# Expert results added straight into the rows of the residual sums, and a last stage that only copies

## The reference, cut to what matters

```
out = x + attention(xn)                      # 16 heads of 16, causal, RoPE
        + shared(xn)                         # silu(xn @ sgate.T) * (xn @ sup.T) @ sdown.T
        + sum over 4 chosen experts of p_e * down_e( silu(gate_e(xn)) * up_e(xn) )
```

## Time and profile before

| | us |
|---|---|
| median of 3 runs (2672.46 to 2676.88) | 2676.68 |
| the profiled execution | 2683.8 |
| its span, first to last instruction | 2681.6 |

### The profile page before, as it was taken

How to read it: one execution, slowest core, us unless ns; L and a number is a source line. 1 busy time by engine, 2 the same in 40 slices (tenths; PEclk the granted TensorE clock), 3 DMA queues, 4 the chain that set the end, 5 groups by cost and what they waited for, 6 DMA issues and landing times. The chain is left out here.

```text
span 2681.6 us, 43680 instructions
## 1 busy us (share of the span) xinstructions
PE 1982.5 (74%) x11279; PEld 1203.6 (45%) x11280; DVE 1349.7 (50%) x3123; ACT 871.7 (33%) x1668; POOL 997.4 (37%) x993
## 2 busy tenths in 40 slices
PE   5778888778788778888777888861888888887700
PEld 2344443334444333443434444330477777776600
DVE  5645546364564545546454454630344444444467
ACT  1323233132322313223232323310255556555500
POOL 4523333432333433233442333446044444444500
PEclk8878888877887877888887887885799999999955
DMA  6052250505325051441505235052544444444389
GB/s 154 25 91 44 60 89 17 100 17 86 51 53 89 22 95 28 75 60 43 98 20 87 43 60 89 22 93 94 175 135 136 136 135 144 138 138 134 101 295 331
DMA packets 217833, 254.99 MB, mean 95 GB/s; under 512 B 74549, under 2 KB 166462, under 8 KB 217664
## 3 DMA queue, kind: packets, MB, share of 16 engines
q1 hardware_dynamic: 160128, 161.90, 28.9%
q0 software_dynamic: 35840, 71.63, 7.8%
q10 hardware_dynamic: 21824, 20.98, 2.5%
HBM read 112.54 MB, written 94.64 MB: 77 GB/s over the span
## 5 line engine op out<-in xcount | busy, mean ns | idle before, releaser
L715 DVE TENSOR_REDUCE neg<-ps_u 128x2 f32<-128x768 f32 (+3 forms) x384 | 392.7, 1044 | 365.9 <-PE ps_u L935 175.5
L494 POOL DMA_INDIRECT table<-entry,slot x256 | 253.8, 991 | 560.9 <-ACT xs L578 462.1
L1207 POOL DMA_INDIRECT y_dram<-yb_all,ent x288 | 283.5, 984 | 327.2 <-ACT yb_all L1163 233.0
L962 PE MATMUL ps_u<-q_st,k_st 50*128 50x512 f32 (+3 forms) x1024 | 205.1, 463 | 188.1 <-DMA q_st<-neg_t 107.4
L915 PE MATMUL ps_g<-we_gu 128*128 128x512 f32 x512 | 263.7, 647 | 60.1 <-DVE hid L702 43.9
L496 POOL DMA_INDIRECT values<-xs,slot x256 | 248.8, 972 | 83.3 <-issue 83.3
L600 ACT ACTIVATE we_d<-ps_u 128x1024 f32<-128x1024 f32 x160 | 163.5, 1023 | 345.0 <-PE ps_u L973 149.7
L931 PE MATMUL ps_u<-k_st,q_st 48*128 48x128 f32 (+3 forms) x1024 | 196.3, 421 | 74.7 <-DVE neg L715 26.2
L481 POOL TENSOR_TENSOR we_d<-we_d 128x512 f32<-128x512 f32 x64 | 81.3, 1270 | 440.8 <-DVE we_d L685 438.0
L962 PEld LDWEIGHTS ps_u<-q_st,k_st 50*128 50x128 f32 x1024 | 106.5, 239 | 290.0 <-issue 113.0
L600 ACT ACTIVATE probs<-ps_u 128x1024 f32<-128x1024 f32 x160 | 161.5, 1022 | 196.2 <-PE ps_u L973 167.4
(11 more groups left out here) (155 smaller groups left out, 3005.6 us busy)
## 6 DMA issues: line engine op xcount, KB each, us to landing
xg<-values SPq DMA_DIRECT2D x288, 128.0 KB
ys<-y_dram SPq DMA_DIRECT2D x64, 512.0 KB, 5.4
q_st<-we_gu SPq DMA_DIRECT2D x192, 128.0 KB
k_st<-we_gu SPq DMA_DIRECT2D x192, 128.0 KB
we_gu<-x SPq DMA_DIRECT2D x16, 512.0 KB
xres<-x SPq DMA_DIRECT2D x16, 512.0 KB
sum_dram<-osum SPq DMA_DIRECT2D x16, 512.0 KB
we_gu<-wgu_e ACTq DMA_DIRECT2D x16, 512.0 KB
```

The source lines that it names most:

```text
L494: pool.indirect_dma_start(table[:, :], bass.IndirectOffsetOnAxis(ap=slot[:, k:k + 1], axis=0), entry[:, k, :], None).then_inc(scattered, 16)
L715: nc.vector.tensor_reduce(neg[:, g % 2, i, :, k0:k0 + nk], ps[:, :, 0:nk * n].rearrange("p a (k n) -> p a k n", n=n), AX.X, ALU.max, negat ...
L962: nc.tensor.matmul(ps[:, a, lo:lo + n], k_st[rows, h, kt * P:(kt + 1) * P], q_st[rows, h, kt * P:SEQ], start=(lo == 0), stop=False, skip_g ...
L1207: pool.indirect_dma_start(y_dram[:, :], bass.IndirectOffsetOnAxis(ap=ent[k][:, 0:1], axis=0), yb[k][:, :], None, bounds_check=TOKENS * TOP ...
```

## The change

The expert rows are no longer kept apart. The residual sums are stored to the first 8192 rows of a new DRAM array `acc`, and each scatter of phase BC adds its rows to them (`compute_op=ALU.add`). The row number in an entry is now the token. Default entries point to 2176 spare rows behind the tokens, which phase A fills with zeros (one more DMA, on SP), and the bounds check is gone. Two blocks of one expert never hold the same token, blocks of different experts can. So POOL now waits before a scatter: for the first 19 blocks until the three scatters before it have landed; for later blocks until the one three earlier has landed, and where `apart[n]` is 16 (the block is the first of its expert, or one of those left over) for the two between as well. `apart` is made by five more operations in the plan, and POOL reads it into a register for each block. SP no longer loads the sums in phase BC. Phase D is 16 loads of 512 KB from `acc` into 16 buffers, issued by SP, and 16 stores of the same buffers to `out`, issued by ACT as each lands; VectorE has nothing to do there.

```diff
+SPARE = -(-(P + TABLE // P - 1) // P) * P
...
-    sum_dram = nc.dram_tensor("sum_dram", (TOKENS, D), F32, kind="Internal").ap()
+    acc = nc.dram_tensor("acc", (TOKENS + SPARE, D), F32, kind="Internal").ap()
     table = nc.dram_tensor("table", (TABLE, 2), I32, kind="Internal").ap()
-    y_dram = nc.dram_tensor("y_dram", (TOKENS * TOPK, D), F32, kind="Internal").ap()
...
-                    sp.dma_start(tokens(sum_dram, b), osum[:, :, :]).then_inc(sum_out, 16)
+                    sp.dma_start(tokens(acc, b), osum[:, :, :]).then_inc(sum_out, 16)
...
+                    sp.wait_ge(consts, N_EARLY)
+                    sp.dma_start(acc[TOKENS:TOKENS + SPARE, :].rearrange("(k p) d -> p k d", p=P),
+                                 zeros[:].rearrange("p (o d) -> p o d", o=1).broadcast_to([P, SPARE // P, D])
+                                 ).then_inc(spare_set, 16)
             run(sp, {"loaded": loaded, "stack": stack_rows, "gate": gate, "negT": neg_store, "oproj": store})
             sp.wait_ge(sum_out, 16 * BATCH)
+            sp.wait_ge(spare_set, 16)
...
-            const(pool.iota(dest_f[:], pattern=[[P * TOPK, NT], [1, TOPK]], base=0, channel_multiplier=TOPK,
+            const(pool.iota(dest_f[:], pattern=[[P, NT], [0, TOPK]], base=0, channel_multiplier=1,
...
-                    pool.memset(blank.rearrange("p (r c) -> p r c", c=2)[:, :, 0:1], SKIP).then_inc(inited, 1)
+                    pool.iota(blank.rearrange("p (r c) -> p r c", c=2)[:, :, 0], pattern=[[1, TABLE // P]], base=TOKENS,
+                              channel_multiplier=1).then_inc(inited, 1)
...
-                back.link(b, nc.vector.tensor_scalar(dest_f[:], dest_f[:], float(SEQ * TOPK), None, ALU.add))
+                back.link(b, nc.vector.tensor_scalar(dest_f[:], dest_f[:], float(SEQ), None, ALU.add))
...
+        FLIGHT = 3
...
-            def sums_part(i):
-
-                nt = TOKENS // P // LOOPS
-                sp.dma_start(sums[:, bass.ds(i * nt, nt), :],
-                             sum_dram.rearrange("(t p) d -> p t d", p=P)[:, bass.ds(i * nt, nt), :]
-                             ).then_inc(sums_in, 16)
-            expert_loop(sp, stage, sums_part)
-            sp.wait_ge(sums_in, 16 * LOOPS)
+            expert_loop(sp, stage)
...
-            def scatter(n, k, first):
+            def scatter(n, k):
+
+
+                static = isinstance(n, int) and n < NR + FLIGHT
+                if not static:
+                    other = pool.value_load(apart[0:1, bass.ds(n, 1)], min_val=0, max_val=16)
+                for back in range(1, FLIGHT + 1):
+                    if isinstance(n, int) and n < back:
+                        continue
+                    kb = (k - back) % NR
+                    past = (n - back - kb) * (16 // NR)
+                    pool.wait_ge(y_out[kb], past + 16 if static or back == FLIGHT else past + other)
                 pool.wait_ge(y_sb, n + 1)
                 hold(pool, passed)
-                pool.indirect_dma_start(y_dram[:, :], bass.IndirectOffsetOnAxis(ap=ent[k][:, 0:1], axis=0),
-                                        yb[k][:, :], None, bounds_check=TOKENS * TOPK - 1, oob_is_err=False
-                                        ).then_inc(y_out[k], 16)
-            expert_loop(pool, scatter)
+                pool.indirect_dma_start(acc[:, :], bass.IndirectOffsetOnAxis(ap=ent[k][:, 0:1], axis=0),
+                                        yb[k][:, :], None, compute_op=ALU.add).then_inc(y_out[k], 16)
+
+            pool.wait_ge(ready, 1)
+            for n in range(2 * NR):
+                scatter(n, n % NR)
+            with pool.Fori(0, LOOPS - 1) as i:
+                for k in range(BODY):
+                    scatter(i * BODY + 2 * NR + k, k)
+            for n in range(NBLOCK - NR, NBLOCK):
+                scatter(n, n % NR)
...
+            link(nc.vector.tensor_copy(row_f[:, 1, :], ps_g[0][0:1, 0:NBLOCK]))
+            link(nc.vector.tensor_tensor(row_f[:, 2, 1:NBLOCK], row_f[:, 1, 1:NBLOCK], row_f[:, 1, 0:NBLOCK - 1],
+                                         ALU.not_equal))
+            link(nc.vector.scalar_tensor_tensor(out=row_f[:, 2, 1:NBLOCK], in0=row_f[:, 1, 1:NBLOCK], scalar=float(E),
+                                                in1=row_f[:, 2, 1:NBLOCK], op0=ALU.is_ge, op1=ALU.max))
+            link(nc.vector.tensor_scalar(row_f[:, 1, 1:NBLOCK], row_f[:, 2, 1:NBLOCK], 16.0, None, ALU.mult))
+            link(nc.vector.tensor_copy(apart[:, 1:NBLOCK], row_f[:, 1, 1:NBLOCK]))
...
-def phase_d(nc, sb_, sem, y_dram, sums, out):
+def phase_d(nc, sb_, sem, acc, out):
     stack = ExitStack()
     with stack:
-        NTILE = TOKENS // P
-        ND = 4
-        ys = [sb_(f"ys{i}", [P, TOPK, D], F32, stack) for i in range(ND)]
-        red = [sb_(f"red{i}", [P, 2, D], F32, stack) for i in range(ND)]
-        res = [sb_(f"res{i}", [P, D], F32, stack) for i in range(ND)]
-        y_in = [sem(f"y_in{i}") for i in range(ND)]
-        stored = [sem(f"stored{i}") for i in range(ND)]
-        half, added = sem("half"), sem("added")
-        added_p, half_p = sem("added_p"), sem("half_p")
+        PIECES = 16
+        rows = TOKENS // PIECES
+        held = [sb_(f"held{i}", [P, rows // P, D], F32, stack) for i in range(PIECES)]
+        held_in = [sem(f"held_in{i}") for i in range(PIECES)]
+        stored = sem("stored")
         block = stack.enter_context(nc.Block())
-        y_v = y_dram.rearrange("(n p j) d -> n p j d", p=P, j=TOPK)
-
-        def tiles(eng, stage):
-            for n in range(ND):
-                stage(n, n, True)
-            with eng.Fori(1, NTILE // ND) as i:
-                for k in range(ND):
-                    stage(i * ND + k, k, False)
+
+        def piece(dram, k):
+            return dram[k * rows:(k + 1) * rows, :].rearrange("(p t) d -> p t d", p=P)
         @block.sync
         def _(sp):
-            def load(n, k, first):
-                if not first:
-                    sp.wait_ge(added, n - ND + 1)
-                sp.dma_start(ys[k][:, :, :], y_dram[bass.ds(n * (P * TOPK), P * TOPK), :].rearrange(
-                    "(p j) d -> p j d", j=TOPK)).then_inc(y_in[k], 16)
-            tiles(sp, load)
+            for k in range(PIECES):
+                sp.dma_start(held[k][:, :, :], piece(acc, k)).then_inc(held_in[k], 16)
         @block.scalar
         def _(act):
-            def store(n, k, first):
-                act.wait_ge(added, n + 1)
-                act.dma_start(out[bass.ds(n * P, P), :], res[k][:, :]).then_inc(stored[k], 16)
-            tiles(act, store)
-            for k in range(ND):
-                act.wait_ge(stored[k], 16 * NTILE // ND)
-
-        @block.vector
-        def _(dve):
-            def add(n, k, first):
-                dve.wait_ge(y_in[k], (n - k) * (16 // ND) + 16)
-                if not first:
-                    dve.wait_ge(added, n - ND + 1)
-                nc.vector.tensor_tensor(red[k][:], ys[k][:, 0:2, :], ys[k][:, 2:4, :], ALU.add).then_inc(half, 1)
-                dve.wait_ge(half, 2 * n + 1)
-                nc.vector.tensor_tensor(red[k][:, 0, :], red[k][:, 0, :], red[k][:, 1, :], ALU.add).then_inc(half, 1)
-                dve.wait_ge(half, 2 * n + 2)
-                if not first:
-                    dve.wait_ge(stored[k], (n - k) * (16 // ND))
-                nc.vector.tensor_tensor(res[k][:], red[k][:, 0, :],
-                                        sums[:, bass.ds(n, 1), :].rearrange("p o d -> p (o d)"), ALU.add).then_inc(added, 1)
-            tiles(dve, add)
+            for k in range(PIECES):
+                act.wait_ge(held_in[k], 16)
+                act.dma_start(piece(out, k), held[k][:, :, :]).then_inc(stored, 16)
+            act.wait_ge(stored, 16 * PIECES)
```

More of the change, by code:

```diff
@@ L188, in block_kernel @@
         phase_a(nc, sb, sem, ident, identb, iota_e, counts, we_gu, we_d, ps_g, ps_u, ps_av, x, wqkvr, wgu_e, wd_e, wo, wgu_s, wd_s, bias,
-                rope_cos, rope_sin, values, sum_dram, table)
-        phase_bcd(nc, sb, sem, ident, iota_e, counts, we_gu, we_d, ps_g, ps_u, ps_av, values, sum_dram, table,
-                  y_dram, out)
+                rope_cos, rope_sin, values, acc, table)
+        phase_bcd(nc, sb, sem, ident, iota_e, counts, we_gu, we_d, ps_g, ps_u, ps_av, values, acc, table, out)
 def phase_a(nc, sb_, sem, ident, identb, iota_e, counts, we_gu, we_d, ps_g, ps_u, ps_av, x, wqkvr, wgu_e, wd_e, wo, wgu_s, wd_s, bias,
-            rope_cos, rope_sin, values, sum_dram, table):
+            rope_cos, rope_sin, values, acc, table):
     stack = ExitStack()
@@ L297, in phase_a @@
         consts, w_front, weights, inited, table_set = sem("consts"), sem("w_front"), sem("weights"), sem("inited"), sem("table_set")
[L298 removed]
+        xs_ready, slots, spare_set = sem("xs_ready"), sem("slots"), sem("spare_set")
         x_in, x_res, sum_out = sem("x_in"), sem("x_res"), sem("sum_out")
@@ L1039, in _, with phase_bcd, phase_bc @@
```

(14 more changed lines are left out.)

## The result

The changed kernel takes 2744.85 us (median of 4, 2728.29 to 2748.82) against 2676.78 us: the ratio is 1.0246, with an interval of 1.0209 to 1.0282. It is slower, by 68 us, where I had forecast 23 us less.

What follows compares the result with a forecast made beforehand. Transfers were taken to bound phase D, SP's issue pace phase BC. Phase D -73.5, chains +62.6, SP's relief -15, plan +2 and phase A +1 gave -23 us: 2654 us, 8-in-10 range 2611 to 2728.

Steps and rivals of the forecast that it cites:

- three signs of being wrong: C above 4.6 us, phase D staying above 65 us, or SP's middle pace changing by more than 0.1 us a block.
- C: Time from one scatter to the next where each waits for the one before: 4.0 us forecast, bounds 3.25 to 6.
- POOL's own work doesn't bind: Middle of phase BC: queued scatters start 1.29 us apart, so waits between the chains cost zero, hidden by 15 us of slack.
- L: Time from a scatter's start on POOL to its landing: about 2.3 us before, 3.05 us forecast with the add.
- 3.5C: Time an expert's scatters take in the middle of phase BC, said to stay below 17.4 us of arrivals until C = 5.0.
- rival 3: Slower, the chain becomes the bound: above C = 4.63 us; 2724 us at C = 5.2; chance 0.22 with rival 4 included.
- The first chain, 19C - 48.8: First 19 blocks of phase BC: delay of SP through late buffer reuse, +27 us at C = 4.0, not won back.
- The last chain: Last 16 blocks of phase BC, fillers: 17C - 32.6 added, +35 us at C = 4.0.
- SP's relief, -15: Phase BC: SP without 16 loads of the sums saves 1 us for each, -15 us, bounds 0 and -30.
- Phase D, -73.5: Phase D moves 16.8 MB at 2.78 us each plus ends: 51 us against 124.6, bounds 47 to 65 us.
- Phase A, +1: Phase A: zeros on SP's queue ahead of loads of x, and the ramp for the fill: +1 us, bounds 0 and 8.
- Rivals 1, 2 and 4: 1: add nearly free, 2624 us, 0.24. 2: no SP relief, 2669 us, 0.12. 4: waits wrong, over 500 us more, under 1 in 50.

Runs made afterwards that it cites:

- e3: Changed kernel with adding scatters to rows of their own, no waits for landings, expert rows left out of the output: 2071.6 us, 0.992 of before.
- e8: Changed kernel with fillers dropped and not waited for, and only block 9 of the first 19 in a chain: 2163.8 us, 1.037 of before.
- e2: Changed kernel with compute_op taken out, so scatters overwrite instead of adding, with the same waits and rows: 2121.0 us.
- e7: Changed kernel where, of the first 19 blocks, only block 9 waits for all three before it: 2216.1 us.
- e6: Changed kernel with filler rows dropped by a bounds check and the last 16 blocks not waiting one by one: 2213.0 us.
- e1: Changed kernel with plain scatters to rows apart, no waits for landings, expert rows left out of the output: 2015.7 us, 0.966 of before.
- e4: Kernel before, unedited, run again on another chip: 2079.7 us.
- e5: Changed kernel, unedited, on a faster chip than the first: 2262.3 us, 1.085 of before.
- e10: Changed kernel with six scatters in flight in place of three: 2271.8 us, 1.089 of before.
- e9: Changed kernel with odd experts adding into a second array, fillers dropped, waits only for the scatter three back: 2091.8 us, 1.001 of before.
- e11: Kernel before with expert rows in bfloat16 and PE adding the four rows in phase D: 2020.8 us, 0.969 of before.

## Why the prediction was wrong

The order of the argument held: phase D is a question of bytes, the chains are the price, and which of them is larger decides. It failed in sizes, and in one step that was wrong in kind. The forecast was missed by 91 us: 57 in the middle, 25 in the first chain, 9 at the end of phase BC and 7 ahead of its first scatter, while phase D gave 7 more than forecast. Two of the prediction's own three signs of being wrong came: C is above 4.6 us, and the middle's pace moved by more than 0.1 us, from 2.08 to 2.25.

1. **"POOL's own work doesn't bind: queued scatters start 1.29 us apart."** This is the step that failed. It took the plain scatter's occupancy for an operation that the trace didn't contain, and gave it no bounds, while L got some. Measured: 1.557 us busy and 1.86 from start to start. The text had the threshold, 17.4 us of arrivals for an expert. With 8.4 blocks of the middle, 7.4 x 1.86 + 5.1 at the border (568.4 - 223 x 1.862 = 153 us over 30 borders) are 18.9 us. So the middle cost +42 us in place of nothing, and where blocks are faster +150. The larger C wasn't the reason: 3.5C at the measured 4.7 is 16.5 us, still under 17.4. e3 and e8 separate the two on the faster chips: 54 us for POOL's pace, 90 us for the borders. On the first chip neither was run; there the same spacings stand in the timeline, and blocks arrive 2.08 us apart, so POOL's 1.86 us alone wouldn't bind and only together with the borders does it.
2. **C = 4.0 us.** Measured 4.68 to 4.75 in the two chains of the first trace, 4.5 to 4.6 in their calm stretches. The plain part was right (3.25, measured 3.23 in e2); the add was set at 0.75 and is 1.4. Of the 0.75 only the 0.34 us for the read came from a row; for the pairing and the return of the read there was none. POOL's part of the 1.4, 0.6 us, had been put at nothing. C went past the 4.63 that rival 3 named for the change of sign, but only just: with C = 4.7 alone the prediction's sum gives +2 us, not +68.
3. **The first chain, 19C - 48.8.** With the measured C the formula gives 40; it cost 52. It granted POOL the slack of the ring before SP is held. That slack is of use only if POOL catches up later, and by point 1 it never does. e7 shows it: the whole chain comes back as time, 46 us.
4. **The last chain** was right in mechanism and short by C: +45.5 for the intervals against 35 with the landing. The landing itself is 1.2 us later (3.5 us after the start in place of 2.3), yet the whole way from the last scatter to phase D became 1.4 us shorter, which isn't explained. e6 gets 49 us.
5. **SP's relief, -15.** Nothing in e1 against e4 (416.9 against 417.3), where PE is the bound. On the first chip it can't be told: the scatters hide it. The reading was too thin: SP's pauses of the earlier trace rows stand beside the load of the sums, and like ones stand where there is none. Between 2000 and 2500 the trace before has 132 intervals of more than 1 us from one issue of SP to the next, 283 us together; 15 of them, 45 us, begin with such a load.
6. **Phase D, -73.5**, measured -80.5. Loads and stores, each with 4 KB to a partition, ran at 388 GB/s over the window where before had 337. The lower bound of 47 us had the old price for a MB; the new one is 43.2 x 0.98 / 16.8 = 2.5 us.
7. **Phase A, +1.** Its first batch is later by 4.8 us: the store of the first sums is issued at 166.03 and was at 161.23. Behind the zeros the issue of the next load of x takes 15.97 us, where it took 0.46 before:

```profile
43.42 0.46 SPq L425 DMA_DIRECT2D acc<-zeros  x1
43.92 15.97 SPq L402 DMA_DIRECT2D xres<-x  x1
59.94 1.27 SPq L396 DMA_DIRECT2D we_gu<-x  x1
```

   Over the rest of the phase the profiled execution gained 18 us, while e5, whose first scatter comes 10.9 us later than e4's, lost another 6. The other runs point the same way without proving it: in the eight with the zeros at the head (e1 to e3, e5 to e8, e10) the first scatter comes at 1477 to 1491 us, in the three without them there (e4, e9, e11) at 1469 to 1472. I have no run that separates this from what one execution differs from another, and leave it open.

Rival 3 was the case that came true in sign, at 0.22. Its time for C = 5.2 was 2724; the time came with C = 4.7, because a slower POOL wasn't in any case; that its sign came true owes as much to this term as to its own. Rivals 1, 2 and 4 are out. The range, up to 2728, missed by 17 us for the same reason.

## What to carry to other kernels

An operation that the trace doesn't contain has as many unknown prices as it has resources: its time on the issuing engine, its time on the transfer engines and its latency; each needs both bounds, and the engine's occupancy must be held against the pace of the loop that it joins. Where order is kept by waiting for landings, count the steps of the chain (here 34 forced ones and 30 borders) and multiply by the full round trip, and grant no slack for them unless the engine that is delayed can run faster than the rest afterwards. And first ask what bounds the stage that is to be relieved: it was bytes, and halving those of the expert rows gave 66 us without any chain.

## What the runs showed of the hardware

- A scatter of 128 rows of 1 KB that adds has 144 packets, 9 for each engine, where a copy has 48. It takes 1.56 us of POOL in place of 0.96 to 0.98, also when every row of it is dropped, and 1.14 us of 16 engines in place of 0.34. The prediction cited the Trainium skill (Collectives: The Full Stack, "The bandwidth ceiling: the fold count and why AG ≠ RS ≠ AR") for an add that costs one more read and nothing else; the page measured it on collectives. The moving time here is 3.3 times that of a copy and not 2, and a scatter costs POOL 0.6 us more; for rows of 1 KB scattered by POOL the measurement decides against the rule's factor.
- The same program took 2677 us on one chip and 2085 to 2087 on three others. The granted clock over the span was 0.83 and 0.91 to 0.93, and blocks of phase BC took 2.08 and 1.65 us at a granted clock of 0.98 and 1.00; the stretches bound by POOL and by landings agreed within 1%. So the clock granted to TensorE doesn't explain the pace of the blocks. The traces show where the time goes: in the middle of phase BC PE waits for `xg` on the first chip (15 us on PE and 28 us on its weight loads) and not at all in e4, and SP's issues have the pauses of point 5, 132 above 1 us in 500 us against 66 in 400 us in e4. Why SP's issues pause more there is open.
- Transfers of phase D with 4 KB to a partition in both directions ran at 413 to 425 GB/s in their steady stretch and at a mean of 388, where phase D before had a mean of 337.
